# Graph network on one core: VectorE's steps of the last edge stage in a new order, message parts read in place, four of eight one-hots on ScalarE

## The reference

```python
# h: LayerNorm and ReLU of x, 50000 x 16; edge_attr 850000 x 48; edge_vec 850000 x 3
s, v = s0[dst], v0[dst]                       # 16 scalars and 4 vectors of the edge's node
w = relu(edge_attr @ fc1_w1 + fc1_b1) @ fc1_w2 + fc1_b2
wa = w[:, :256].reshape(E, 16, 16)
wb = w[:, 256:].reshape(E, 4, 16)
path_a = einsum('ei,eij->ej', s, wa)
path_b = einsum('eic,ec,eij->ej', v, sh1, wb) / sqrt(3)
msg = (path_a + path_b) / sqrt(20)
node1 = bn_scalar(segment_mean(msg, src))     # then x + node1
```

## Time and profile before

| | |
|---|---|
| median of three runs | 23958.75 us |
| lowest and highest | 23958.6 and 23959.51 us |
| span of the profiled execution | 23994.0 us |
| own device time of that execution | not given apart from its span |
| VectorE busy | 19509.6 us (81%) |
| GpSimd busy | 15973.0 us (67%) |
| TensorE matmuls busy | 15946.4 us (66%) |
| ScalarE busy | 10304.8 us (43%) |
| mean granted TensorE clock | 0.791 |

### The profile page before, as it was taken

How to read it: one execution, slowest core, us unless ns; L and a number is a source line. 1 busy time by engine, 2 the same in 40 slices (tenths; PEclk the granted TensorE clock), 3 DMA queues, 4 the chain that set the end, 5 groups by cost and what they waited for, 6 DMA issues and landing times.

```text
span 23994.0 us, 483073 instructions
## 1 busy us (share of the span) xinstructions
PE 15946.4 (66%) x137837; PEld 9487.0 (40%) x137837; DVE 19509.6 (81%) x37328; ACT 10304.8 (43%) x23410; POOL 15973.0 (67%) x18227
## 2 busy tenths in 40 slices
PE   5232777777777777766666577766777777777675
PEld 2221333333333333335656333333343333433333
DVE  8114888888888888889999888888888888888888
ACT  1001444444444444449999433333333333333332
POOL 0772777777777777777777566666666666666665
PEclk6555888888888888877777788888888888888887
DMA  4223333333333333324444222121222222222221
GB/s 142 52 50 132 111 111 106 110 111 111 106 109 111 111 107 109 111 97 118 118 118 118 65 40 40 40 40 40 40 40 40 40 40 40 40 40 40 40 40 37
DMA packets 1355296, 1864.35 MB, mean 78 GB/s; under 512 B 497379, under 2 KB 1137507, under 8 KB 1298789
## 3 DMA queue, kind: packets, MB, share of 16 engines
q1 hardware_dynamic: 835620, 1342.87, 18.2%
q0 software_dynamic: 483776, 469.85, 9.2%
q10 hardware_dynamic: 35842, 50.96, 0.6%
HBM read 1452.58 MB, written 409.77 MB: 78 GB/s over the span
## 4 chain that ended last, share of the span: by engine, by line
DVE 42%; issue 23%; POOL 16%; DVEq 6%; DMA 4%; ACT 3%; PE 3%; ACTq 1%; POOLq 1%; SPq 0%
POOL rows_d L731 13%; DVE arena L1767 11%; DVE arena L1716 7%; DVE arena L1774 6%; DVE arena L1758 5%; DMA rows_d<-arena 4%; DVEq L1794 4%; POOL arena L622 3%; DVE arena L1723 3%; ACT arena L1204 2%; DVE arena L1789 2%; DVE arena L1649 1%; DVE arena L1748 1%; DVE arena L1751 1%; PE wide L978 1%
## 5 line engine op out<-in xcount | busy, mean ns | idle before, releaser
L622 POOL DMA_INDIRECT arena<-s_tab,arena x7072 | 6703.2, 948 | 3772.1 <-issue 2032.1
L731 POOL DMA_INDIRECT rows_d<-arena x6656 | 6424.9, 965 | 2426.7 <-issue 2309.7
L1053 PE MATMUL wide<-w,arena 64*128 64x320 f32 x14144 | 3202.5, 546 | 2843.6 <-DVE arena L1758 2840.6
L978 PE MATMUL wide<-w,arena 64*128 64x320 f32 x13312 | 2975.3, 536 | 2257.1 <-DVE arena L1640 1639.7
L1649 DVE TENSOR_REDUCE arena<-arena 128x40 f32<-128x640 f32 x3328 | 2693.5, 809 | 428.3 <-DMA rows_d<-arena 427.6
L1640 DVE TENSOR_TENSOR arena<-wide,arena 128x640 f32<-128x640 f32 x3328 | 2653.0, 818 | 235.8 <-PE wide L978 167.0
L1053 PEld LDWEIGHTS wide<-w,arena 64*128 64x128 f32 x14144 | 1265.6, 210 | 3954.1 <-issue 2198.5
L1758 DVE TENSOR_TENSOR arena<-wide,arena 128x640 f32<-128x640 f32 x3536 | 2807.3, 815 | 0.2 <-PE wide L1053 0.2
L1767 DVE TENSOR_REDUCE arena<-arena 128x32 f32<-128x640 f32 x3536 | 2780.7, 806 | 0.0
L978 PEld LDWEIGHTS wide<-w,arena 64*128 64x128 f32 x13312 | 1189.1, 209 | 3150.7 <-issue 1778.3
L1039 PEld LDWEIGHTS duo<-ident_sb,arena 128*64 128x64 f32 x14144 | 1623.4, 175 | 1107.9 <-issue 1107.9
(11 more groups left out here) (208 smaller groups left out, 26899.6 us busy)
## 6 DMA issues: line engine op xcount, KB each, us to landing
arena<-rows_d SPq DMA_DIRECT2D x3536, 172.0 KB, 2.3
arena<-in_attr SPq DMA_DIRECT2D x208, 1024.0 KB
arena<-rel SPq DMA_DIRECT2D x208, 1024.0 KB
arena<-in_attr_rows SPq DMA_DIRECT2D x208, 768.0 KB
arena<-s_tab,arena POOLq DMA_INDIRECT x7072
rows_d<-arena POOLq DMA_INDIRECT x6656
rows_d<-zero ACTq DMA_DIRECT2D x198, 172.0 KB, 1.8
side<-arena SPq DMA_DIRECT2D x16, 1040.0 KB
```

What stands on the lines that cost most here:

```text
L622: pool.indirect_dma_start(out=dst_, out_offset=None, in_=tab, in_offset=bass.IndirectOffsetOnAxis(ap=idx, axis=0)).then_inc(signal, 16)
L731: pool.indirect_dma_start(out=rows_d[t // 4], out_offset=bass.IndirectOffsetOnAxis(ap=ui[:, s % GPT, t:t + 1], axis=0), in_=M[:, s % GPT, ...
L978: last = pe.matmul(wide[k % 2][:, j, 0:WN], hT[half, s % 2, k * P:(k + 1) * P], w2_sb[0][half, :], start=True, stop=True)
L1053: last = pe.matmul(wide[k % 2][:, j, 0:WN], bhT[half, s % 2, k * P:(k + 1) * P], w2_sb[1][half, :], start=True, stop=True)
```

## The change

In `back` alone:

1. **VectorE's order.** The vector product and its reduction for g+1 (`turn_vectors`, `vectors`) are made in group g, around the last reduction. The two bins' numbers are loaded ahead of the join (`bins_of`); `join` of g-2 stands ahead of the one-hots; its two adds stand behind the reductions 2 and 3. The waits for all reductions and one-hots ahead of the join are gone, and the releases of buffers go by semaphores of the steps themselves (`vec_terms`, `hot`, `hot_dve`, `prod`).
2. **Parts in place.** The messages lie as [tile][part][16] in fp32. Part q's bf16 is the upper half of the fp32 word (`bupper`), read with a step of two bf16. The rests subtract that from the word. Both casts of ScalarE are gone, and `nodes` reads `bupper`.
3. **One-hots.** VectorE makes four of eight tiles instead of six, ScalarE four instead of two; ScalarE's squares stand ahead of the copy of the attributes.

```diff
-DVE_TOO = 6
+BACK_DVE = 4
...
-        bmsg = v[5].rearrange("p (s t c) -> p s t c", s=2, t=TPG)
-        brest = v[6].rearrange("p (s t c) -> p s t c", s=2, t=TPG)
-        bparts = v[7].bitcast(BF16).rearrange("p (s t q c) -> p s t q c", s=2, t=TPG, q=3)
...
+        bmsg = v[5].rearrange("p (s t q c) -> p s t q c", s=2, t=TPG, q=3)
+        bupper = v[5].bitcast(BF16).rearrange("p (s t q c w) -> p s t q c w", s=2, t=TPG, q=3, w=2)[:, :, :, :, :, 1]
...
                         if not first:
-                            sp.wait_ge(R.rows_free, g - (GPT - 1))
-                            sp.wait_ge(R.hot_too, g - (GPT - 1))
+                            sp.wait_ge(R.vec_terms, g - (GPT - 1))
+                            sp.wait_ge(R.hot, g - (GPT - 1))
+                            sp.wait_ge(R.hot_dve, g - (GPT - 1))
                             sp.wait_ge(R.turned, g - (GPT - 1))
...
                         if not first:
-                            pool.wait_ge(R.x_free, g - (GPT - 1))
+                            pool.wait_ge(R.prod, 4 * g - 4 * (GPT - 1))
...
                                 last = pe.matmul(pair[:, s % 2, at:at + 3 * NS], bhot[:, s % 2, 4 * h + t, m * P:(m + 1) * P],
-                                                 bparts[:, s % 2, 4 * h + t, :, :].rearrange("p q c -> p (q c)"), start=t == 0, stop=t == 3)
+                                                 bupper[:, s % 2, 4 * h + t, :, :].rearrange("p q c -> p (q c)"), start=t == 0, stop=t == 3)
...
                 def body(it, first, last):
                     for s in range(GPT):
                         g = it * GPT + s
-                        f = first and s == 0
-                        if not f:
-                            cast0(g - 1, (s - 1) % GPT, first and s < 3)
                         if not (last and s == GPT - 1):
-                            relu(g + 1, (s + 1) % GPT, f)
-                        if not f:
-                            cast1(g - 1, (s - 1) % GPT)
+                            relu(g + 1, (s + 1) % GPT, first and s == 0)
+                        squares(g, s, it)
                         if not (last and s + 2 >= GPT):
                             copy_attr(g + 2, (s + 2) % GPT)
-                        squares(g, s, it)
                         hot_nodes(g, s, first and s < 2)
...
-                def prepare(g, s, it):
+                def turn_vectors(g, s, it):
                     dve.wait_ge(R.gathered[s], 16 * TPG * it + 16 * TPG)
...
+                def vectors(g, s):
+                    dve.wait_ge(R.vec_terms, g + 1)
                     red(bxg[:, s, :, 28:32], vtmp, AX, ALU.add).then_inc(R.vec, 1)
...
+                def rest0(g, s, first):
+                    dve.wait_ge(R.red, 4 * g + 4)
+                    if not first:
+                        dve.wait_ge(R.summed, g - 1)
+                    tt(bmsg[:, s % 2, :, 1, :], bmsg[:, s % 2, :, 0, :], bupper[:, s % 2, :, 0, :], ALU.subtract).then_inc(R.rest, 1)
...
+                def bins_of(g):
+                    return [dve.value_load(bin_sb[0:1, bass.ds(g + h * 8 * P, 1)], min_val=0, max_val=NB - 1) for h in range(2)]
+
+                def join(g, s, first):
                     dve.wait_ge(R.summed, g + 1)
-                    wait_past(dve, R.added, 2 * g)
+                    if not first:
+                        dve.wait_ge(R.added, 2 * g)
                     red(bnew.rearrange("p h (m c) -> p h m c", m=4),
                         pair[:, s % 2, 0:24 * NS].rearrange("p (h m q c) -> p h m c q", h=2, m=4, q=3), AX, ALU.add
                         ).then_inc(R.joined, 1)
...
+                def add(g, h, at):
+                    if h:
+                        dve.wait_ge(R.added, 2 * g + 1)
+                    else:
+                        dve.wait_ge(R.joined, g + 1)
+                    own = into[:, bass.ds(at * (4 * NS), 4 * NS)]
+                    tt(own, own, bnew[:, h, :], ALU.add).then_inc(R.added, 1)
+
+                def body(it, first, last):
                     for s in range(GPT):
                         g = it * GPT + s
                         f = first and s == 0
-                        before = (s - 1) % GPT
-                        prepare(g, s, it)
+                        before, two = (s - 1) % GPT, (s - 2) % GPT
+                        joins = not (first and s < 2)
+                        more = not (last and s == GPT - 1)
+                        multiply(g, s, 0, f)
                         if not f:
-                            rest0(g - 1, before)
-                        multiply(g, s, 0, f)
+                            rest0(g - 1, before, first and s < 3)
                         multiply(g, s, 1, f)
                         reduce_(g, s, 0, first and s < 2)
                         if not f:
                             rest1(g - 1, before)
                         multiply(g, s, 2, f)
                         reduce_(g, s, 1, False)
-                        hot_nodes(g, s, first and s < 2)
+                        if joins:
+                            at = bins_of(g - 2)
+                            join(g - 2, two, first and s < 3)
+                        hot_nodes(g, s, it, first and s < 2)
                         multiply(g, s, 3, f)
                         reduce_(g, s, 2, False)
+                        if joins:
+                            add(g - 2, 0, at[0])
+                        if more:
+                            turn_vectors(g + 1, (s + 1) % GPT, it + (s + 1) // GPT)
                         reduce_(g, s, 3, False)
-                        dve.wait_ge(R.red, 4 * g + 4)
-                        dve.wait_ge(R.hot, g + 1)
-                        dve.sem_inc(R.x_free, 1)
-                        dve.sem_inc(R.rows_free, 1)
-                        if not (first and s < 2):
-                            add(g - 2, (s - 2) % GPT)
+                        if joins:
+                            add(g - 2, 1, at[1])
+                        if more:
+                            vectors(g + 1, (s + 1) % GPT)
```

More of the change, by code:

```diff
@@ L1315, in relu @@
                     act.activation(bhT[:, s % 2, :], banks[0][:, :], ACT.Relu, bias=b1_sb[1][:, :]).then_inc(R.relu, 1)
[L1317 to L1320, removed]
-                    act.copy(bparts[:, s % 2, :, 0], bmsg[:, s % 2]).then_inc(R.cast0, 1)
-                def cast1(g, s):
-                    act.wait_ge(R.rest, g + 1)
-                    act.copy(bparts[:, s % 2, :, 1], brest[:, s % 2]).then_inc(R.cast1, 1)
                 def squares(g, s, it):
                     act.wait_ge(R.ld[s], 32 * it + 32)
-                    wait_past(act, R.hot_too, g)
-                    for t in range(DVE_TOO, TPG):
-                        last = act.activation(bsq[:, t - DVE_TOO, :], ids512[:, :], ACT.Square, scale=-1.0, bias=brow[:, s, t, 0:1])
+                    wait_past(act, R.hot, g)
+                    for t in range(BACK_DVE, TPG):
+                        last = act.activation(bsq[:, t - BACK_DVE, :], ids512[:, :], ACT.Square, scale=-1.0, bias=brow[:, s, t, 0:1])
                     last.then_inc(R.squared, 1)
@@ L1337, in hot_nodes @@
                         act.wait_ge(R.summed, g - 1)
-                    act.activation(bhot[:, s % 2, DVE_TOO:TPG, :], bsq, ACT.Relu, scale=-1.0, bias=ones[:, 0:1]).then_inc(R.hot_too, 1)
+                    act.activation(bhot[:, s % 2, BACK_DVE:TPG, :], bsq, ACT.Relu, scale=-1.0, bias=ones[:, 0:1]).then_inc(R.hot, 1)
                 def body(it, first, last):
@@ L1791, in add @@
                         ).then_inc(R.joined, 1)
-                    dve.wait_ge(R.joined, g + 1)
-                    for h in range(2):
-                        at = dve.value_load(bin_sb[0:1, bass.ds(g + h * 8 * P, 1)], min_val=0, max_val=NB - 1)
-                        if h:
-                            dve.wait_ge(R.added, 2 * g + 1)
-                        own = into[:, bass.ds(at * (4 * NS), 4 * NS)]
-                        tt(own, own, bnew[:, h, :], ALU.add).then_inc(R.added, 1)
-                def body(it, first):
+                def add(g, h, at):
[6 more added lines that the diff above has]
+                def body(it, first, last):
                     for s in range(GPT):
@@ L1814, in body @@
                         reduce_(g, s, 1, False)
-                        hot_nodes(g, s, first and s < 2)
+                        if joins:
+                            at = bins_of(g - 2)
+                            join(g - 2, two, first and s < 3)
+                        hot_nodes(g, s, it, first and s < 2)
                         multiply(g, s, 3, f)
                         reduce_(g, s, 2, False)
+                        if joins:
+                            add(g - 2, 0, at[0])
+                        if more:
+                            turn_vectors(g + 1, (s + 1) % GPT, it + (s + 1) // GPT)
                         reduce_(g, s, 3, False)
-                        dve.wait_ge(R.red, 4 * g + 4)
```

(27 more changed lines are left out.)

50 lines of the change are left out of this document (20 added, 30 removed).

## The result

The changed kernel takes **22472.14 us** (median of 4 runs, 22469.18 to 22473.3) against 23958.67 us, a ratio of 0.938 with the interval 0.9367 to 0.9393: 1486.5 us less. Measured again it took 22477.31 us, 0.9381 (0.9366 to 0.9397). Predicted were 22475 us and 1486.6 less.

The account below looks back on a forecast made before the run. GpSimd's eight gathers, 10.03 us a group, were to bound the changed kernel: 883 steps, 8856.5 us, plus the stage's end, finish 1486.6 us earlier. Taken from the median 23958.75 this gave 22475 us, range 22425 to 22950.

Parts of the forecast that it names:

- The bound: Last edge stage: GpSimd's eight gathers at 1.2535 us set the pace, 10.03 us a group; chance 0.62.
- The waits of 1.9 us: VectorE's idle time a group before the join and before each of its two adds; predicted to lose its cause.
- VectorE alone: VectorE's own work a group in the changed kernel, without waits for other engines: 9.3 us, under GpSimd's 10.03.
- The one-hots: Two of VectorE's six one-hots a group go to ScalarE: 0.57 us less on VectorE.
- the circle: TensorE and VectorE waiting on each other, third multiply through weights 2: 9.8 us a group; as pace-setter, chance 0.28.
- x: TensorE's part of the circle, weights 1, hidden and transposes: 3.38, 4.98 or 6.26 us by clock, mean 4.9.
- The loads: Register loads of both bin numbers on VectorE's queue ahead of the join: taken as nothing, bounds 0 and 0.6 us.
- The half words: Rests and node sums reading bf16 halves at a 4-byte step: taken as nothing; slower node sums had chance 0.04.
- The relu of 2048 columns: ScalarE's one-hot relu, doubled from 1024 columns: 2.0 us, within 6.0 us of ScalarE work a group, hidden.
- The sum: 883 steps of 10.03 us, 8856.5 us, plus the stage's end: 1486.6 us less, 22475 us for the whole kernel.

Follow-up runs that it names:

- the two forms with six one-hots: Changed kernel with six one-hots on VectorE: parts in place, 23167.58 us; parts in own buffers with both casts on ScalarE, 23174.28 us.
- the three other kernels that ran there: Changed kernel with casts on ScalarE, 1.07; kernel before with four one-hots on VectorE, 1.0775; changed kernel with six and weights 0 made three times, 1.0835.

## Why the prediction was right

**The bound.** GpSimd's eight gathers at 1.2535 us, 10.03 us a group, seen at the start of the old kernel: measured 10.02, and shown as the bound by one gather more and one less.

**The waits and the two one-hots.** The waits of 1.9 us are gone; the one before the second add, which I had read as some 0.6 us, was 0.71 in the trace. VectorE alone was put at 9.3 us; an undisturbed group with four one-hots took 8.76. The one-hots were mis-sized: six took 1.72 us in the group of the earlier trace rows, but 1.80 in that kernel's mean and 1.85 in the kernel with six, so four save 0.7 of the circle instead of 0.57, and x another 0.5. It didn't matter to the sum, since GpSimd's floor cut both off.

**The loads.** Taken as nothing, between 0 and 0.6 us; measured 0.06 to 0.08. The Trainium skill's floor for a tensor load (DMA: Bandwidth & Descriptors, Latency and other measured facts) would have left 0.2 open; the trace has each load at 0.30 us and doesn't agree.

**The half words.** Taken as nothing: node sums 0.97 for 0.98 us, and no difference in time between the two forms with six one-hots. The Trainium skill's rule on strides within a line (SBUF — State Buffer, Door 1) agrees.

**ScalarE.** The relu of 2048 columns was put at 2.0 us and took 2.00; hidden.

**The circle.** Taken as 9.8 us, with x at 4.9; 9.70 with seven gathers, with x at 4.7. The margin to GpSimd was thin indeed, 0.32 us: with two one-hots more the circle is the bound, at 10.81.

**The sum.** 883 steps took 8851.6 us (22370.7 - 13519.1) against 8856.5, the end 15.8 against 15.6. The 35 us between the span of the profile before and the median of its runs were left out of the difference, which was right: they lay ahead of the last stage, which began 32 us earlier in the changed kernel's profile (13519.1 against 13551.6 us) though nothing there was changed, and the changed kernel's profiled span, 22469.5, is close to its runs. That the difference came out at 1486.5 for 1486.6 is luck to a part: the pace alone was off by 5 us.

## What to carry to other kernels

Look for what comes right under the bound that a change removes, and read its pace where it already shows: at a stage's start, before the old bound has set in, two rows gave the new period to 0.1%. When an engine's idle stretch served as cover for another's chain, count the circle through both; here it lay 0.3 us under the new bound. Work that makes TensorE wait can cost more than its own length: here 1.1 us in the circle for 0.7 of one-hots. And where chips differ, a gain on one kind is no gain on the other until it is timed there.

## What the runs showed of the hardware that was not expected

With six one-hots TensorE had both its longest idle spells and its lowest granted clock:

```profile
PE wide L1050 <- DVE arena L1740: 1739.5, 648, 2.9
```

1739.5 / 648 = 2.7 us once a group, all of it ahead of weights 1, and 36% of the time at 1.2 GHz. In the changed kernel all weights together waited 1522.7 / 698 = 2.2 us a group, 2.04 of it ahead of weights 1, and it was 28%. But the spell's length alone doesn't give the clock. With seven gathers TensorE waited less than in the changed kernel, 1.99 us a group, and had 30% at 1.2 GHz:

```profile
14000.00:21000.00 7000.00, 5528.81 (x47642) 3220.37 (x47638) 6269.59 (x13704) 3973.65 (x5053) 4788.11 (x5051) 0.85 0.23 47
```

And the kernel before has 34% in the earlier trace rows, with 2.1 us in the two middle groups of the earlier trace rows. So the clock is a part of the price of work on this circle, and the runs don't say by which rule.

On four of six chips TensorE got its instructions one at a time in two of four groups: matmuls of 0.3 us at 0.7 and 1.4 us from one another (the rows above from 20013.56 on). VectorE then stood still for 7.79 us (20020.15 above) and 15.96 us (20029.37 with the casts back). The traces are those of the edited kernels; the kernel before has none from such a chip. It took 28500 to 29100 us there instead of 23960, and the three other kernels that ran there took 1.07 to 1.08 of that, the kernel before with two one-hots moved among them. None of the three was timed where instructions came in time. The rows show the gaps, not their cause, and the runs leave open why these kernels lose more to them than the kernel before.

Two loads of a register with the steps around them take 1.1 us of VectorE's queue. Between a join and its adds they left VectorE idle for 0.85 and 0.71 us; behind a multiply and a reduction they cost 0.06 to 0.08 us in all. The trace shows them run beside these: in the group above the first load starts at 18005.01, 0.08 us after the third multiply, and the second at 18005.73, 0.06 us after the reduction.
